# Graph network kernel: layer norm of y for every second dense step moved to where y is made

## The chip, the cores and the metric

The kernel runs on one core of a Trainium2 chip. A core has TensorE (PE), VectorE (DVE), ScalarE (ACT), GpSimd (POOL) and SyncE (SP, which here only issues DMAs), each with its own queue of instructions, and 16 DMA engines. The metric is the device time of one execution in microseconds (us); lower is better.

## The reference

Four graph layers follow one another on 50,000 nodes with 128 features, each as `x = layernorm(x + layer(x))`. The third layer, around which the change lies, is a two-step mean aggregation over 25,000 edges:

```python
def _sage(x, src, dst, Wl, b, Wr):
    m = _mean_aggr(x, src, dst, x.shape[0])
    return m @ Wl.T + b + x @ Wr.T
...
h = jax.nn.relu(_sage(x, src, dst, W1l, b1, W1r))
out = _sage(h, src, dst, W2l, b2, W2r)
...
x = _layernorm(x + _L2_gnn_ref(x, edge_index, 0, ...), axis=-1)
```

For a node that no edge ends in, the mean is zero, so its new value needs no gather: h1 = relu(x2 W1r + b1), y = x2 + h1 W2r + b2, x3 = layernorm(y).

## The kernel before, in words

Every layer treats the nodes twice. **Dense steps** compute all 50,000 nodes as if no edge ended in them: 49 steps of 128 x 8 rows, the last with 106 partitions. **Edge steps** compute the rows for the 25,000 edges, 49 steps of 128 x 4. Each table (x1, x2, h1, x3) is a DRAM tensor with the edge rows first (`SLOTS` rows) and the node rows behind them.

Each engine runs its own program. `pipeline(eng, looped, stages)` writes it: at iteration s it calls, in the order in which they are listed, all stages with their lag; a stage with lag 3 works on step s - 3. The order of the list is the order of the work on that engine, and nothing else reorders it; the engines meet by semaphores only (`wait_done`, `wait_free`, `wait_previous`, `wait_landed`, `wait_drained`). Buffers have two halves, by the step's parity `g.b`, and DMAs are counted on one semaphore for each half (`Ring`).

**The node stage** (layers `x2` and `nodes2`). One iteration makes x2 for a dense step and an edge step. SP loads node_sums and node_in (L648, L577), DVE adds the means into node_in and takes the moments (`make_x2`: L1862, L1499, L1505), ACT the root (L1197), DVE the inverse root and the shift (L1530, L1516), ACT writes the normed rows node_out (L1211) and new_rows for the edges. Two iterations later, PE transposes node_out (L1037), ACT copies it out (node_x2t, L1312), PE multiplies by W1r (L1044, the h1 product), ACT applies relu (node_h1t, L1319), PE transposes h1 back (L1063) and multiplies by W2r (L1055), ACT copies h1's rows (node_h, L1327), DVE adds ps and node_out to node_y (`nodes_y`, L1890). SP stores x2, h1 and y (L584, L654, L659); y goes to a table of its own, `y_nodes`. POOL gathers sums for the edge step (L760).

**The first aggregation** (layers `sage1` and `nodes3`). POOL gathers x2 rows (L768), DVE makes running sums and means (L1552, L1908), PE transposes and multiplies, ACT copies t_a and t_b (L1220), applies relu (L1347) and writes h1 rows (L1352). One dense step is woven into each edge step: SP loads y (L577), DVE takes moments and shifts, ACT writes eight normed rows, SP stores them to the node part of the x3 table. **The second aggregation** (`sage2`) has edge steps only.

The stages of the node stage on ACT, in this order:

```python
pipeline(act, DENSE_FULL, [
    nodes(3, nodes_copy_x2t), nodes(4, nodes_copy_h1), nodes(3, nodes_relu),
    nodes(2, normed_rows(D, "n", node_in, node_out, "n_row", "n_out", ("x2tp", "y")))]
    + edges((2, normed_rows(L, "e", pre, new_rows, "newd", "stored")))
    + [nodes(1, roots(D, "n"))] + edges((1, roots(L, "e"))))
```

## Time and profile before

| | |
|---|---|
| median of 3 runs | 3004.59 us (3003.99 to 3005.47) |
| profiled execution | 3004.84 us, its span 3003.0 us |
| PE, DVE, ACT, POOL busy, whole span | 60%, 74%, 67%, 63% |
| mean granted clock of PE | 0.772 |
| moved by DMA | 663.86 MB, 221 GB/s in the mean |

The shares of the whole span are means over stages with different limits, so a stage is read by itself: first its busy times in a window, then who waits for whom in it, then the timeline of an engine over a step. In a timeline, a row is a run of equal instructions on one engine with start, duration, and in brackets how long the engine was idle before it and what ended that. Durations overlap the next instruction's start a little; the distance between starts is what a run costs.

### The profile page before, as it was taken

To read this page: it belongs to the slowest core of one execution; us is meant where nothing else is said; L and a number is where in the kernel's file an instruction comes from. 1 tells how busy PE (TensorE), PEld (TensorE's weight loads), DVE (VectorE), ACT (ScalarE), POOL (GpSimd) and SP (SyncE) were. 2 spreads that over 40 slices of the span, in tenths; PEclk is the share of its full clock that TensorE was granted. 3 is DMA by queue.
4 is the path that set the end of the run, shared out by engine and by line. 5 is a ranking of instruction groups with operands and counts; after the bars stand their busy time and mean duration, and the time that the engine had idled before them with its cause. 6 is when DMAs were issued, how large, how long until landed. Compare 5 with 4: busy or idle time off the path is not lost. (4 is left out here: it accounts for less than half of the span.)

```text
span 3003.0 us, 51944 instructions
## 1 busy us (share of the span) xinstructions
PE 1805.3 (60%) x9371; PEld 1338.1 (45%) x9371; DVE 2230.8 (74%) x8474; ACT 2022.7 (67%) x5239; POOL 1891.8 (63%) x1802
## 2 busy tenths in 40 slices
PE   5666666444455443677777667666665666635552
PEld 4565655233333332445555433335554555524442
DVE  7978888766666663787878566666886888888883
ACT  5888878444344432788888688883554888858885
POOL 7777776588888886333333465537775766426775
PEclk8877777677767776798999888887998888755555
DMA  6989988333333333899999799996886888834441
GB/s 210 304 287 298 301 292 278 96 63 62 59 62 62 62 62 71 278 348 340 348 337 350 268 332 329 324 310 199 257 259 196 295 293 287 271 122 160 159 159 50
DMA packets 293472, 663.86 MB, mean 221 GB/s; under 512 B 55177, under 2 KB 88596, under 8 KB 293404
## 3 DMA queue, kind: packets, MB, share of 16 engines
q1 hardware_dynamic: 214587, 549.74, 52.8%
q0 software_dynamic: 78816, 113.45, 17.3%
q14 instruction: 55, 0.44, 0.0%
q8 instruction: 14, 0.23, 0.0%
HBM read 342.83 MB, written 324.08 MB: 222 GB/s over the span
## 5 line engine op out<-in xcount | busy, mean ns | idle before, releaser
L1211 ACT ACTIVATE node_out<-node_in,n_shift,n_root 128x128 f32<-128x128 f32 (+1 forms) x1176 | 468.2, 482 | 75.5 <-DVE n_shift L1516 74.6
L760 POOL DMA_INDIRECT sums<-gat_sums,dst_safe_i x196 | 185.1, 945 | 292.1 <-DVE pre L1862 237.8
L827 POOL DMA_INDIRECT gat_sums<-sums,add_idx x196 | 322.4, 1645 | 66.6 <-issue 58.5
L1499 DVE BATCH_NORM_STATS2 n_stats<-node_in 128x6 f32<-128x256 f32 (+1 forms) x784 | 279.2, 418 | 82.0 <-DMA node_in<-y_nodes 69.1
L880 POOL DMA_INDIRECT out_dram<-node_x2t,out_index x196 | 211.1, 1077 | 167.9 <-ACT node_x2t L1211 107.6
L768 POOL DMA_INDIRECT src_rows<-x_table,row_i x200 | 197.5, 988 | 134.3 <-issue 53.2
L768 POOL DMA_INDIRECT sums<-x_table,row_i x192 | 193.7, 1009 | 99.5 <-issue 50.0
L760 POOL DMA_INDIRECT own_rows<-x_table,row_i x196 | 191.1, 975 | 65.8 <-issue 54.2
L768 POOL DMA_INDIRECT own_rows<-in_x_dram,dst_safe_i x196 | 192.6, 983 | 59.7 <-issue 56.4
L760 POOL DMA_INDIRECT src_rows<-in_x_dram,src_i x196 | 191.1, 975 | 60.2 <-issue 58.7
L1220 ACT ACTIVATE t_a<-ps 128x512 f32<-128x512 f32 (+1 forms) x198 | 116.1, 587 | 149.3 <-PE ps L924 149.1
L1002 PE MATMUL ps<-node_h,msg 128*128 128x512 f32 (+1 forms) x200 | 111.6, 734 | 145.6 <-DVE node_h L1792 145.6
L1002 PE MATMUL ps<-node_y,msg 128*128 128x512 f32 (+1 forms) x192 | 106.2, 729 | 152.3 <-DVE node_y L1792 152.3
L1211 ACT ACTIVATE new_rows<-pre,e_shift,e_root 128x128 f32<-128x128 f32 x393 | 161.4, 484 | 15.1 <-DMA x_table<-new_rows 12.6
L1220 ACT ACTIVATE t_b<-ps 128x512 f32<-128x512 f32 (+1 forms) x198 | 116.0, 586 | 71.6 <-PE ps L924 71.5
L924 PE MATMUL ps<-ident,own_rows 128*128 128x128 f32 x588 | 100.4, 299 | 93.8 <-DMA own_rows<-in_x_dram,dst_safe_i 87.4
L1211 ACT ACTIVATE node_out<-node_in,n_shift,both_root 128x128 f32<-128x128 f32 (+1 forms) x392 | 156.2, 495 | 0.3 <-DVE n_shift L1516 0.3
L924 PE MATMUL ps<-ident,msg 128*128 128x128 f32 x590 | 106.1, 307 | 81.8 <-DVE msg L1908 65.2
L1002 PEld LDWEIGHTS ps<-node_h,msg 128*128 128x128 f32 x200 | 60.5, 318 | 195.3 <-issue 172.2
L1815 DVE TENSOR_TENSOR add_idx<-key,dummy_rows 128x4 int32<-128x4 f32 x49 | 8.0, 164 | 187.6 <-DMA gat_sums<-sums,add_idx 187.4
L1002 PEld LDWEIGHTS ps<-node_y,msg 128*128 128x128 f32 x192 | 57.9, 317 | 199.2 <-issue 187.2
L924 PEld LDWEIGHTS ps<-ident,msg 128*128 128x128 f32 x590 | 76.3, 158 | 140.9 <-issue 94.3
(359 smaller groups left out, 6548.7 us busy)
## 6 DMA issues: line engine op xcount, KB each, us to landing
x_table<-node_out SPq DMA_DIRECT2D x144, 512.0 KB
own_rows<-x_table SPq DMA_DIRECT2D x245, 256.0 KB, 3.0
node_in<-x_table SPq DMA_DIRECT2D x96, 512.0 KB
acc_dump<-acc SPq DMA_DIRECT2D x147, 264.0 KB
x_table<-new_rows SPq DMA_DIRECT2D x147, 256.0 KB
gat_sums<-node_x2t SPq DMA_DIRECT2D x49, 528.0 KB
node_sums<-gat_sums SPq DMA_DIRECT2D x48, 528.0 KB
node_in<-in_x_dram SPq DMA_DIRECT2D x48, 512.0 KB
```

Source lines behind the costliest of these rows:

```text
L760: g_.indirect_dma_start(out=to[:, g.b, j, 0:width], out_offset=None, in_=tab, in_offset=bass.IndirectOffsetOnAxis(ap=indices(j), axis=0)). ...
L768: g_.indirect_dma_start(out=to4[g.q][:, j, 0:F], out_offset=None, in_=tab, in_offset=bass.IndirectOffsetOnAxis(ap=indices(j), axis=0)).the ...
L827: g_.indirect_dma_start(out=gat_sums[:, :], out_offset=bass.IndirectOffsetOnAxis(ap=add_idx[:, g.b, j:j + 1], axis=0), in_=sums[:, g.b, j, ...
L880: g_.indirect_dma_start(out=out[:, :], out_offset=bass.IndirectOffsetOnAxis(ap=out_index[:, t:t + 1], axis=0), in_=wide_new[:, g.b, j, :], ...
L924: last = te.transpose(ps[bank][g.b][:, j * F:(j + 1) * F], tiles[:, j, 0:F], ident[:, :])
L1002: te.matmul(ps[2][g.b][:, 0:n], msg[:, g.b, j, 0:F], same[g.b][:, j, 0:n], start=j == J - 1, stop=j == 0)
L1211: last = sc.activation(to[0:pn, g.b, j, :], rows[0:pn, g.b, j, 0:F], ACT.Identity, bias=NORM[k][2][0:pn, g.b, j:j + 1], scale=root[0:pn, j ...
L1220: sc.activation(to[:, g.b, 0:jn * F], ps[bank][g.b][:, 0:jn * F], ACT.Copy).then_inc(L[copied].sem, 1)
L1499: last = v.bn_stats(NORM[k][0][0:pn, g.b, j:j + 2, :].rearrange("p j c -> p (j c)"), rows[0:pn, g.b, j:j + 2, 0:F].rearrange("p j f -> p f ...
L1815: v.tensor_tensor(add_idx[:, g.b, :], key4[:, g.b, 4, :], dummy_rows[:, :], ALU.add).then_inc(L["rep2"].sem, 1)
```

## The change

Every second dense step (0, 2, ... 48: 25 "even" steps) gets its layer norm in the node stage, from node_y in SBUF, and is stored straight to the x3 table instead of to `y_nodes`. The other 24 steps go to `y_nodes` as before, and only these are loaded, normed and stored in the first aggregation, one in two iterations. The result of the even norm goes to the buffer `gate`, which is free in both stages. The moments of an even step stand on DVE behind its `nodes_y`; the root, the shift and the eight rows follow an iteration later, the rows at the end of ACT's iteration, ahead of the roots. SP stores them at the head of the iteration behind that. `pipeline` learns stages at half rate, the loops of the first aggregation on SP and ACT are unrolled by four instead of two (DVE's was already), and the stages behind wait for the even stores as well.

```diff
     def at(s):
-        for lag, stage, count in stages:
-            if 0 <= s - lag < count:
-                stage(step(s - lag))
+        for lag, stage, count, *half in stages:
+            t = s - lag
+            if half and t >= 0 and t % 2 == 0 and t // 2 < count:
+                stage(step(t // 2))
+            elif not half and 0 <= t < count:
+                stage(step(t))
...
+def even_only(stage):
+    def make(g):
+        if g.b == 0:
+            stage(g, Even(g.k, 0))
+    return make
...
+            "even3": dict(front=norm("m") + ["m_row"], rings={}, steps=EVEN_STEPS),
-            "nodes3": dict(front=norm("n") + ["n_row"], rings=dict(n_in=1, n_out=1), steps=DENSE_STEPS),
+            "nodes3": dict(front=norm("n") + ["n_row"], rings=dict(n_in=1, n_out=1), steps=ODD_STEPS),
...
+        x3_even = gate[:, :, :, :].rearrange("p b j f -> p (b j) f")
...
             def store_y(g):
+                if g.b == 0:
+                    return
                 wait_done(sp, D["y"], g)
...
+            def store_even_x3(g, e):
+                wait_done(sp, flow["even3"]["m_row"], e)
+                for lo, hi in parts(g):
+                    sp.dma_start(node_rows(x3_table, SLOTS, g)[lo:hi], x3_even[lo:hi]).then_inc(even3_out, 16)
...
-            pipeline(sp, DENSE_FULL, [nodes(5, store_h1), nodes(5, store_y), nodes(3, store_nodes(D, x2_table, SLOTS))]
+            pipeline(sp, DENSE_FULL, [nodes(6, even_only(store_even_x3)), nodes(5, store_h1), nodes(5, store_y), nodes(3, store_nodes(D, x2_table, SLOTS))]
...
-                     + [nodes(0, load_nodes(D, y_nodes, 0, "n_row"))] + edges((1, dump))
-                     + [nodes(2, store_nodes(D, x3_table, SLOTS))] + edges((3, store)))
+                     + [odd_nodes(0, load_odd_y)] + edges((1, dump)) + [odd_nodes(2, store_odd_x3)] + edges((3, store)), per=4)
...
+            def even_root(g, e):
+                wait_done(act, M["m_ve"], e)
+                at = NORM["m"][1][0:dense_p(g), 0, :]
+                sc.activation(at, at, ACT.Sqrt).then_inc(M["m_rt"].sem, 1)
+
+            def even_x3(g, e):
+                pn = dense_p(g)
+                if not e.first_use():
+                    act.wait_ge(even3_out, 16 * e.k)
+                wait_done(act, M["m_nm"], e)
+                for j in range(DJ):
+                    last = sc.activation(x3_even[0:pn, j, :], node_y[0:pn, 0, j, :], ACT.Identity,
+                                         bias=NORM["m"][2][0:pn, 0, j:j + 1], scale=NORM["m"][1][0:pn, 0, j:j + 1])
+                last.then_inc(M["m_row"].sem, 1)
+
             pipeline(act, DENSE_FULL, [
-                nodes(3, nodes_copy_x2t), nodes(4, nodes_copy_h1), nodes(3, nodes_relu),
+                nodes(3, nodes_copy_x2t), nodes(5, even_only(even_root)), nodes(4, nodes_copy_h1), nodes(3, nodes_relu),
...
-                + [nodes(1, roots(D, "n"))] + edges((1, roots(L, "e"))))
+                + [nodes(5, even_only(even_x3)), nodes(1, roots(D, "n"))] + edges((1, roots(L, "e"))))
...
-            pipeline(act, DENSE_FULL, [nodes(1, roots(D, "n"))] + edges((2, h1_rows))
-                     + [nodes(1, normed_rows(D, "n", node_in, node_out, "n_row", "n_out"))]
-                     + edges((1, sage_relu), (0, sage_copies)))
+            pipeline(act, DENSE_FULL, [odd_nodes(1, roots(D, "n"))] + edges((2, h1_rows))
+                     + [odd_nodes(1, normed_rows(D, "n", node_in, node_out, "n_row", "n_out"))]
+                     + edges((1, sage_relu), (0, sage_copies)), per=4)
...
-                wait_drained(dve, D["n_y"], g)
+                if g.b:
+                    wait_drained(dve, D["n_y"], g)
+                else:
+                    wait_previous(dve, flow["even3"]["m_row"], Even(g.k, 0))
...
-            pipeline(dve, DENSE_FULL, [nodes(2, shifts(D, "n"))] + edges((2, shifts(L, "e"))) + [nodes(4, nodes_y)]
-                     + edges((1, make_x2)))
+            def even_shifts(g, e):
+                pn, at = dense_p(g), NORM["m"][1][0:dense_p(g), 0, :]
+                wait_done(dve, M["m_rt"], e)
+                v.reciprocal(at, at).then_inc(M["m_rc"].sem, 1)
+                wait_done(dve, M["m_rc"], e)
+                shift_of(M, "m", e, pn, DJ, at)
+
+            def even_moments(g, e):
+                pn = dense_p(g)
+                wait_done(dve, D["y"], g)
+                wait_previous(dve, M["m_row"], e)
+                stats(M, "m", e, node_y, pn, DJ)
+                variances(M, "m", e, pn, DJ, NORM["m"][1][:, 0, :])
+
+            pipeline(dve, DENSE_FULL, [nodes(2, shifts(D, "n"))] + edges((2, shifts(L, "e"))) + [nodes(5, even_only(even_shifts))]
+                     + [nodes(4, nodes_y), nodes(4, even_only(even_moments))] + edges((1, make_x2)))
...
-            pipeline(dve, DENSE_FULL, edges((0, plain_sums)) + [nodes(1, shifts(D, "n"))] + edges((0, means))
-                     + [nodes(0, node_moments(D))], per=4)
+            pipeline(dve, DENSE_FULL, edges((0, plain_sums)) + [odd_nodes(1, shifts(D, "n"))] + edges((0, means))
+                     + [odd_nodes(0, node_moments(D))], per=4)
```

Line numbers in the orders below are those of each program by itself: L1211 of before is L1267 of the change. The first place is ACT in the node stage, one iteration near its end, before:

```order
L1312 ACTIVATE node_x2t<-ps 128x512 x2
L1327 ACTIVATE node_h<-ps 128x512 x2
L1319 ACTIVATE node_h1t<-ps,cols 128x512 x2
L1211 ACTIVATE node_out<-node_in,n_shift,n_root 128x128 x8
L1211 ACTIVATE new_rows<-pre,e_shift,e_root 128x128 x4
L1197 ACTIVATE n_root<-n_root 106x8
L1197 ACTIVATE e_root<-e_root 128x4
```

and in the change, an iteration with an even step (m_root and gate are the root and the result of the even norm):

```order
L1368 ACTIVATE node_x2t<-ps 128x512 x2
L1392 ACTIVATE m_root<-m_root 128x8
L1383 ACTIVATE node_h<-ps 128x512 x2
L1375 ACTIVATE node_h1t<-ps,cols 128x512 x2
L1267 ACTIVATE node_out<-node_in,n_shift,n_root 128x128 x8
L1267 ACTIVATE new_rows<-pre,e_shift,e_root 128x128 x4
L1400 ACTIVATE gate<-node_y,m_shift,m_root 128x128 x8
L1253 ACTIVATE n_root<-n_root 106x8
L1253 ACTIVATE e_root<-e_root 128x4
```

One root came in behind the x2t copy, and eight row operations between new_rows and the roots.

The second place is DVE in the same stage, in the iteration in which an even y is made, of the change:

```order
L1966 TENSOR_TENSOR node_y<-ps,node_out 128x512 x2
L1572 BN_STATS m_stats<-node_y 128x6 x4
L1578 TENSOR_SCALAR m_root<-m_stats 128x8
L1923 TENSOR_REDUCE node_recip<-node_sums 128x8
L1923 TENSOR_REDUCE edge<-sums 128x4
L1928 TENSOR_SCALAR node_recip<-node_recip 128x8
L1928 TENSOR_SCALAR edge<-edge 128x4
L1931 RECIPROCAL node_recip<-node_recip 128x8
L1931 RECIPROCAL edge<-edge 128x4
L1935 SCALAR_TENSOR_TENSOR node_in<-node_sums,node_recip,node_in 128x128 x8
L1935 SCALAR_TENSOR_TENSOR pre<-sums,edge,own_rows 128x128 x4
```

The two lines with m_stats are new; the rows from node_recip on are `make_x2`, which stood directly behind node_y before.

The third place is ACT in the first aggregation, before:

```order
L1197 ACTIVATE n_root<-n_root 128x8
L1352 ACTIVATE new_rows<-ps 128x512
L1211 ACTIVATE node_out<-node_in,n_shift,n_root 128x128 x8
L1347 ACTIVATE t_c<-ps,cols 128x512
L1220 ACTIVATE t_a<-ps 128x512
L1220 ACTIVATE t_b<-ps 128x512
L1197 ACTIVATE n_root<-n_root 128x8
L1352 ACTIVATE new_rows<-ps 128x512
```

and in the change, over two iterations:

```order
L1276 ACTIVATE t_a<-ps 128x512
L1276 ACTIVATE t_b<-ps 128x512
L1425 ACTIVATE new_rows<-ps 128x512
L1420 ACTIVATE t_c<-ps,cols 128x512
L1276 ACTIVATE t_a<-ps 128x512
L1276 ACTIVATE t_b<-ps 128x512
L1253 ACTIVATE n_root<-n_root 128x8
L1425 ACTIVATE new_rows<-ps 128x512
L1267 ACTIVATE node_out<-node_in,n_shift,n_root 128x128 x8
```

The dense step's root and its eight rows (L1267) stand in every second iteration only.

## Rows read from the trace of the kernel before

**Rows 1.** Windows of three stages: us, busy per engine, clock, DMA share, GB/s

```profile
1234.60:1690.00 455.40, 343.43 (x1755) 237.24 (x1754) 367.28 (x1448) 375.92 (x921) 163.19 (x173) 0.92 0.96 343
1710.40:2019.40 309.00, 215.06 (x767) 113.70 (x768) 208.13 (x773) 259.34 (x624) 172.04 (x182) 0.85 0.95 323
2044.00:2290.00 246.00, 170.60 (x1181) 140.36 (x1179) 200.71 (x750) 129.97 (x323) 180.81 (x190) 0.96 0.80 248
```

**Rows 2.** Tile node_y: form, count, ns min/median/max, first and last start

```profile
L1890 DVE TENSOR_TENSOR node_y<-ps,node_out x98: 678/681/692, 1224.0 to 1698.4; 128x512 f32<-128x512 f32 x96, 106x512 f32<-106x512 f32 x2
```

**Rows 3.** Timeline of ACT, first aggregation's first and last t_b: start, us, operation

```profile
1710.41 0.60 ACT L1220 ACTIVATE t_b<-ps 128x512 f32<-128x512 f32 x1 [6.95 <-PE ps L924]
...
2019.36 0.58 ACT L1220 ACTIVATE t_b<-ps 128x512 f32<-128x512 f32 x1
```

**Rows 4.** Waits, 1250 to 1650 us: total us, times, longest

```profile
ACT node_h1t L1319 <- PE ps L1044: 47.3, 40, 2.8
DVE node_recip L1850 <- DMA node_in<-x_table: 43.3, 31, 2.5
...
ACT n_root L1197 <- DVE n_root L1505: 15.5, 17, 1.8
```

**Rows 5.** Timeline of ACT, one node step

```profile
1442.08 0.20 ACT L1197 ACTIVATE n_root<-n_root 128x8 f32<-128x8 f32 x1
...
1442.37 1.08 ACT L1312 ACTIVATE node_x2t<-ps 128x512 f32<-128x512 f32 x2
1443.34 1.09 ACT L1327 ACTIVATE node_h<-ps 128x512 f32<-128x512 f32 x2
1445.53 1.26 ACT L1319 ACTIVATE node_h1t<-ps,cols 128x512 f32<-128x512 f32 x2 [1.09 <-PE ps L1044]
1446.68 3.17 ACT L1211 ACTIVATE node_out<-node_in,n_shift,n_root 128x128 f32<-128x128 f32 x8
1449.76 1.64 ACT L1211 ACTIVATE new_rows<-pre,e_shift,e_root 128x128 f32<-128x128 f32 x4
```

**Rows 6.** Timeline of DVE, one node step, and ACT's root in it

```profile
1409.44 1.43 DVE L1499 BATCH_NORM_STATS2 n_stats<-node_in 128x6 f32<-128x256 f32 x4
1410.79 0.74 DVE L1499 BATCH_NORM_STATS2 e_stats<-pre 128x6 f32<-128x256 f32 x2
1411.45 0.18 DVE L1505 TENSOR_SCALAR n_root<-n_stats 128x8 f32<-128x8 f32 x1
...
1411.66 0.21 ACT L1197 ACTIVATE n_root<-n_root 128x8 f32<-128x8 f32 x1 [1.23 <-DVE n_root L1505]
...
1420.03 0.18 DVE L1505 TENSOR_SCALAR n_root<-n_stats 128x8 f32<-128x8 f32 x1
```

**Rows 7.** Timeline of PE: transposes (L1063) and h1 products (L1044)

```profile
1409.88 1.04 PE L1063 MATMUL ps<-ident,node_h1t 128*128 128x128 f32 x8
1413.05 3.68 PE L1044 MATMUL ps<-node_x2t,w1r_t 128*128 128x512 f32 x4 [2.13 <-ACT node_x2t L1312]
...
1583.56 1.98 PE L1044 MATMUL ps<-node_x2t,w1r_t 128*128 128x512 f32 x4 [1.61 <-ACT node_x2t L1312]
...
1592.66 1.98 PE L1044 MATMUL ps<-node_x2t,w1r_t 128*128 128x512 f32 x4 [0.73 <-ACT node_x2t L1312]
...
1623.28 1.98 PE L1044 MATMUL ps<-node_x2t,w1r_t 128*128 128x512 f32 x4 [2.94 <-ACT node_x2t L1312]
```

**Rows 8.** DMA issues: count, KB each, us to landing

```profile
y_nodes<-node_y SPq DMA_DIRECT2D x48, 512.0 KB, 6.1
```

**Rows 9.** Timeline of POOL, first gathers of the first aggregation

```profile
1691.75 0.94 POOL L768 DMA_INDIRECT src_rows<-x_table,row_i  x1 [27.91 <-DMA x_table<-new_rows]
1693.00 0.95 POOL L768 DMA_INDIRECT src_rows<-x_table,row_i  x1 [0.30 <-issue]
```

**Rows 10.** Timeline of ACT, second aggregation's first and last t_a

```profile
2044.35 0.60 ACT L1220 ACTIVATE t_a<-ps 128x512 f32<-128x512 f32 x1 [13.81 <-PE ps L924]
...
2293.16 0.60 ACT L1220 ACTIVATE t_a<-ps 128x512 f32<-128x512 f32 x1 [1.57 <-PE ps L924]
```

More of the change, by code:

```diff
@@ L43 @@
 WJ = 7
+ODD_STEPS, EVEN_STEPS = DENSE_STEPS // 2, DENSE_STEPS // 2 + 1
 WIDE_STEPS = T // WJ
@@ L55 @@
 MAGIC = 1597463007.0
-assert FULL_P == P - 1 and 0 < LAST_T < T and T % J == 0 and T % WJ == 0 and DENSE_FULL * P * DJ + TAIL_P * DJ == N_NODES
+assert DENSE_FULL % 2 == 0 and FULL_P == P - 1 and 0 < LAST_T < T and T % J == 0 and T % WJ == 0 and DENSE_FULL * P * DJ + TAIL_P * DJ == N_NODES
 class Step:
@@ L183, in pipeline @@
 def pipeline(eng, looped, stages, per=2):
-    longest = max(lag for lag, _, _ in stages)
+    longest = max(lag for lag, *_ in stages)
     def at(s):
-        for lag, stage, count in stages:
-            if 0 <= s - lag < count:
-                stage(step(s - lag))
+        for lag, stage, count, *half in stages:
[4 more added lines that the diff above has]
+                stage(step(t))
     first = (longest + 3) // 2 * 2 if per == 2 else (longest + 5) // 4 * 4
@@ L198, in pipeline @@
         for h in range(per):
-            for lag, stage, count in stages:
+            for lag, stage, count, *half in stages:
                 if lag + count <= first:
@@ L202, in pipeline @@
                 t = first + h - lag
-                stage(Step(i * (per // 2) + t // 2, t % 2, t % 4, i + t // 4))
-    for s in range(first + per * loops, max(lag + count for lag, _, count in stages)):
+                if not half:
+                    stage(Step(i * (per // 2) + t // 2, t % 2, t % 4, i + t // 4))
+                elif t % 2 == 0:
+                    stage(Step(i + t // 4, t // 2 % 2))
+    for s in range(first + per * loops, max(lag + count * (2 if half else 1) for lag, _, count, *half in stages)):
         at(s)
@@ L224, in wide_edges, with index, odd_nodes @@
     return [(lag, stage, WIDE_STEPS) for lag, stage in stages]
+class Odd(Step):
+    def index(self):
+        return (2 * self.k + self.b) * 2 + 1
+class Even(Step):
+    def index(self):
+        return self.k
+def odd_nodes(lag, stage):
+    return (lag, stage, ODD_STEPS, True)
+def even_only(stage):
[3 more added lines that the diff above has]
+    return make
 def once(lag, stage):
@@ L397, in gnn_program @@
         NORM = {k: (sb(f"{k}_stats", [P, 2, n, 3]), sb(f"{k}_root", [P, 2, n]),
-                    sb(f"{k}_shift", [P, 2, n])) for k, n in (("e", J), ("a", DJ), ("n", DJ))}
+                    sb(f"{k}_shift", [P, 2, n])) for k, n in (("e", J), ("a", DJ), ("n", DJ), ("m", DJ))}
         edge4 = sb("edge4", [P, 2, 6, J])
@@ L472, in gnn_program @@
                     sems[n], counts[n] = sem2(n), [0, 0]
-                flow[layer][n] = Ring(sems[n], counts[n], m, steps, n in ("n_in", "n_out", "n_h1", "n_y"))
+                flow[layer][n] = Ring(sems[n], counts[n], m, steps, n in ("n_in", "n_out", "n_h1", "n_y") and steps == DENSE_STEPS)
                 counts[n] = flow[layer][n].end
@@ L481, in gnn_program @@
                 flow[layer][n] = Signal(sem(n), 0, per)
+        flow["nodes2"]["n_y"].end[0] = 0
+        even3_out = sem("even3_out")
+        EVEN3_STORED = 16 * (EVEN_STEPS - 1 + len(TAIL_PARTS))
+        x3_even = gate[:, :, :, :].rearrange("p b j f -> p (b j) f")
         LAYER_NO = {n: i for i, n in enumerate(("msg", "sage1", "sage2", "att2"))}
@@ L670, in _, with load_odd_y, store_odd_x3 @@
             dump, store = dump_and_store(L, h1_table)
+            def load_odd_y(g):
+                wait_free(sp, D["n_row"], g)
+                sp.dma_start(node_in[:, g.b, :, :], node_rows(y_nodes, 0, Odd(g.k, g.b))).then_inc(D["n_in"].sems[g.b], 16)
+            def store_odd_x3(g):
+                wait_done(sp, D["n_row"], g)
+                sp.dma_start(node_rows(x3_table, SLOTS, Odd(g.k, g.b)), node_out[:, g.b, :, :]).then_inc(D["n_out"].sems[g.b], 16)
             pipeline(sp, DENSE_FULL, edges((0, load_own(L, L["tr_b"], x2_table, own_rows, L["own"])))
-                     + [nodes(0, load_nodes(D, y_nodes, 0, "n_row"))] + edges((1, dump))
-                     + [nodes(2, store_nodes(D, x3_table, SLOTS))] + edges((3, store)))
+                     + [odd_nodes(0, load_odd_y)] + edges((1, dump)) + [odd_nodes(2, store_odd_x3)] + edges((3, store)), per=4)
             L = flow["sage2"]
@@ L689, in _ @@
             wait_all(sp, flow["nodes3"]["n_out"])
+            sp.wait_ge(even3_out, EVEN3_STORED)
             wait_all(sp, flow["sage2"]["stored"])
@@ L864, in _ @@
             wait_all(pool, flow["nodes3"]["n_out"])
+            pool.wait_ge(even3_out, EVEN3_STORED)
             def gather_x3(g):
```

2 lines of the change are left out of this document (added).

## Prediction

> **What bounds the kernel now.** I first read the busy times by stage, because the change touches two stages only [rows 1]. In the first, which makes x2, h1 and y ("node stage", 1234.6 to 1690.0), the 16 DMA engines are busy 96% of the time at 343 GB/s, ACT 376 of 455 us (83%), DVE 367 (81%), PE 343 (75%). In the second, the first aggregation (1710.4 to 2019.4), DMA is at 95% and 323 GB/s, and ACT at 259 of 309 us (84%). The third row is the second aggregation, which has no dense steps beside it: DMA only 80%. By these shares both stages look bound by transfers. Then the length of a step: y is made 49 times, in halves, the first at 1224.0 and the last near 1698.4 [rows 2], so a node step takes 474.4/48 = 9.88 us. The first aggregation does 48 steps between its first and last copy of t_b, (2019.36 - 1710.41)/48 = 6.44 us [rows 3].
>
> Next, what each engine waits for in the node stage, over 400 us or about 40 steps [rows 4]: DVE waits 43.3 us for node_in to land, which is the transfer bound, but ACT also waits 47.3 us for PE's h1 product and only 15.5 us for DVE's variances. ACT's work of 375.92/455.4 x 9.88 = 8.2 us and its wait for PE of 47.3/40 = 1.2 us make 9.4 of the 9.88 us. The wait for PE is no spare room: it lies inside ACT's fixed order. In the timeline of ACT [rows 5] a step runs root, x2t, h copy, then 1.09 us idle while PE multiplies, relu, eight node_out, four new_rows. The shortest distance from one h1 product to the next is 1592.66 - 1583.56 = 9.10 us [rows 7]. That is ACT's own period when nothing else is late. So ACT is within 0.8 us of being the bound in every node step.
>
> **The change, node stage.** Bytes: for an even step the 512 KB store of y becomes a 512 KB store of x3 [rows 8], so the transfers of this stage stay as they are and nothing is gained here. Work is added, once in two steps.
>
> ACT gets one root and eight row operations, in the pipeline's odd iterations. Eight of the same form take 1449.76 - 1446.68 = 3.08 us start to start [rows 5]. The root of about 0.1 us goes into the wait for PE, and costs nothing unless that wait vanishes. Root and Identity already alternate here, and the order shows no table load added. The eight stand between new_rows and the roots for which DVE waits, so an odd iteration takes 9.10 + 3.08 = 12.2 us.
>
> DVE gets four moments and a variance in the even iterations, behind the halves of y and ahead of make_x2. Four moments are 1410.79 - 1409.44 = 1.35 us start to start, the variance with its wait about 0.15, so 1.5. DVE's path from ACT's root to the next variance is 1420.03 - 1411.66 = 8.4 us, and 0.2 more until ACT's root starts (1411.45 to 1411.66) [rows 6]. With 1.5 that is 10.1 us, more than ACT's 9.1. So the even iteration ends at DVE: 10.1 us. DVE's other added work (inverse root and shift, about 0.4 us, behind the wait of about 0.6 for ACT's even root) falls in the odd iteration, where DVE then needs 9.6 of 12.2 us: free.
>
> SP gets a wait for the even x3 at the head of an even iteration, with seven issues queued behind it, the loads for the step among them. Those loads are used an iteration later, and the last of them waits for node_out anyway, so I cost the wait at nothing; its cover is that iteration of 10 us. POOL's gathers of sums gain nothing and lose nothing. DVE's wait for node_in (1.1 us a step) disappears, since x2's loads now have more time; that is already in the periods above. The added wait of DVE's even y on the previous even x3 has ended by then, because ACT's roots stand behind that x3.
>
> An even and an odd iteration take 22.3 us with PE at full clock. After an odd iteration PE stands idle for about 4 us: its transposes end some 2 us behind node_out [rows 7], while new_rows, the eight and x2t fill about 6 us. In this trace the h1 product took 1.98 us in nearly all steps and 3.68 us after an idle gap of 2.13 us, though 1.98 after one of 2.94 [rows 7]: after a gap PE is sometimes at 1.2 instead of 2.4 GHz. A slow product delays ACT by 1.7 us; in the even iteration ACT then needs 10.8 and exceeds DVE by 0.7. I take that half of the time: 22.7 us. Against 19.76 that is 2.94 us, 24 times: **+70.6 us**. Bounds: always full clock 22.3 and small luck, +57; half clock in both iterations 24.1 or so, +95 with some recovery.
>
> The page "TensorE: Matmul & The Clock Gate" of the Trainium skill (section "HAM oscillation — how this bites in real kernels") says that a repeated idle stretch puts the array back to half rate, so that every group starts cold. By that rule each even iteration would start slow, a pair would be 23.0 us and the term +78; this trace agrees only in part, with 3.68 us once and 1.98 us after a longer gap.
>
> **The change, first aggregation.** It loses 25 of 49 loads of y and 25 of 49 stores of x3, 512 KB each: of some 2.1 MB a step (rate times 6.44 us) about a quarter. The rest, 2.08 - 0.53 = 1.55 MB, takes 4.8 us at 323 GB/s. ACT loses 3.2 us and DVE about 1.9 us in every second step. What is next: POOL's gathers come every 1693.00 - 1691.75 = 1.25 us at best [rows 9], four a step, 5.0 us. The nearest row is the second aggregation, with the same gathers and without dense steps: 48 steps from 2044.35 to 2293.16 [rows 10], 5.18 us each. ACT's work without the dense part is 259.34/48 - 3.2 = 2.2 us [rows 1], so steps with dense work need 3.2 + 2.2 and small waits, about 5.5 us, steps without it about 4.6 (copies, PE's product and transposes in a loop); their mean is near 5.1, and POOL's four buffers let them average. Transfers would be at some 93%. I take 5.2: (6.44 - 5.2) x 48 = **-59.4 us**. Bounds: POOL's 196 gathers at 1.25 us from 1691.75 end at 1937, and some 8 us behind them is 1945, so -74; and 5.6 us a step if PE's product takes 3.7 us in the light steps, -40.
>
> **Ends.** Between the stages SP now passes the store of the last even x3 instead of waiting for y; both are due at about the same time. At the end of the aggregation no dense step is in the way of the last relu: **-1.5 us**.
>
> **Sum.** 70.6 - 59.4 - 1.5 = +9.7 us. The profiled execution took 3004.84 us (span 3003.0), 0.25 above the median of 3004.59, and the sum is made against it: 3014.5 us. About 0.2% (6 us) is what a measurement can tell from no change.
>
> **The rivals.**
> (a) *Forecast*: ACT paces the node stage, the aggregation goes to about 5.2 us. Chance 0.45.
> (b) *The other side: ACT's idle time takes up the work.* The node stage stays bound by transfers. ACT's work for two steps would be 2 x 8.2 + 3.2 = 19.6 us, just under the 19.76 that the unchanged bytes need, so the stage costs nothing: 3004.8 - 59.4 - 1.5 = 2944 us; at half of the added time, 2979. It decides where ACT's wait for PE can be filled. Against it: the order puts the eight behind new_rows, not into that wait. Chance 0.08.
> (c) *The gathers set the aggregation*, with PE at full clock: +57 - 74 - 2, 2986 us. For it: the step without dense work in the second aggregation stands at 5.18 with two loads of own rows. Chance 0.12.
> (d) *PE's clock falls more often*, in the node stage (+95) and in part of the light steps (-50): 3004.8 + 95 - 50 - 1.5 = 3048 us. For it: more idle time of PE; the clock is 0.92 in the node stage and 0.85 in the aggregation [rows 1]. Against it: the second aggregation, also with gaps, has 0.96. The rule of the page named above is the mild form of this. Chance 0.20.
> (e) *The aggregation is held by its latencies*, landing of loads and stores, not by bytes: 5.9 us a step, 26 us saved: 3004.8 + 70.6 - 26 - 1.5 = 3048 us. For it: with its period above what PE and ACT need, its waits can re-form. Against it: the 5.18 us of the second aggregation. Chance 0.15.
>
> **How the numbers follow.** Faster by over 0.2%: (b), (c) and a sliver of (a), 0.22. Slower by over 0.2%: (d), (e) and two thirds of (a), 0.64. Within: 0.14. The range runs from (c) to (d) and (e): 2984 to 3050, which leaves out (b) and the worst of (d). The likeliest case's own range is 3003 to 3028.
>
> **What would show it.** The y of the node stage should come alternately some 10.1 to 10.8 and 12.2 us apart, 11.3 in the mean; DVE's wait for node_in should be near nothing; DMA in that stage should fall from 96% to about 85%. The first aggregation should take about 250 us from its first copy to its last instead of 309, with DMA at 90% or more and POOL's idle time mostly "issue". It would be wrong if the node stage kept 9.9 us a step (b), or if the aggregation stayed above 5.6 (d, e).

## Result and profile after

| | before | after |
|---|---|---|
| median of 6 runs each | 3005.32 us (3003.99 to 3019.88) | 3035.8 us (3028.39 to 3041.04) |
| profiled execution, its span | 3004.84, 3003.0 us | 3036.36, 3034.6 us |
| ACT busy, whole span | 2022.7 us | 2016.6 us |
| moved by DMA | 663.86 MB | 637.84 MB |

The ratio after to before is 1.0088 (95%: 1.0069 to 1.0107): slower, by 31.6 us of span between the two profiles, where +9.7 was forecast. The direction held, and ACT's added rows pace the stage as forecast; one term was too small by 24 us. Ratios compare the fast runs alone, medians take in all: now and then an execution ran longer at a lower clock, as did five of the twelve runs of the last kernel of this document, its profiled one among them.

The stages, as windows of the profile of the changed kernel (columns as in [rows 1]):

```profile
1234.60:1785.00 550.40, 390.01 (x1754) 258.83 (x1753) 409.64 (x1607) 444.52 (x1128) 163.66 (x174) 0.82 0.81 284
1804.80:2050.00 245.20, 188.19 (x756) 107.46 (x756) 163.75 (x600) 179.84 (x405) 172.26 (x182) 0.89 0.91 303
```

In the node stage DMA fell from 96 to 81%, ACT went from 83 to 81%, and PE's clock from 0.92 to 0.82: neither transfers nor ACT's own work fill the time. The first aggregation became much shorter, with transfers still at 91%.

The ends of the stages, for [rows 2, 3, 10]: the tile node_y, and copies in the timeline of ACT (start, length):

```profile
L1966 DVE TENSOR_TENSOR node_y<-ps,node_out x98: 680/682/692, 1223.9 to 1792.9; 128x512 f32<-128x512 f32 x96, 106x512 f32<-106x512 f32 x2
```

```profile
1806.43 0.60 ACT L1276 ACTIVATE t_b<-ps 128x512 f32<-128x512 f32 x1 [5.58 <-PE ps L980]
...
2053.17 0.60 ACT L1276 ACTIVATE t_b<-ps 128x512 f32<-128x512 f32 x1
...
2075.13 0.60 ACT L1276 ACTIVATE t_a<-ps 128x512 f32<-128x512 f32 x1 [13.89 <-PE ps L980]
```

From them the balance (each a difference of starts):

| stretch | before | after | difference | forecast |
|---|---|---|---|---|
| first y to last y | 474.4 | 569.0 | +94.6 | +70.6 |
| last y to first t_b | 12.0 | 13.5 | +1.5 | with the next |
| 49th t_b to second aggregation's first t_a | 25.0 | 22.0 | -3.0 | -1.5, both |
| first t_b to 49th t_b | 308.95 | 246.74 | -62.2 | -59.4 |
| sum | | | +30.9 of 31.6 | +9.7 |

The waits from 1250 to 1700 us (total us, times, longest; [rows 4] are of 400 us, these of 450):

```profile
POOL sums L815 <- DVE pre L1935: 263.0, 37, 8.8
...
PE ps L1100 <- ACT node_x2t L1368: 73.9, 33, 3.8
ACT node_h1t L1375 <- PE ps L1100: 63.3, 38, 2.9
DVE n_root L1603 <- ACT n_root L1253: 62.8, 38, 3.2
...
ACT node_x2t L1368 <- PE ps L1093: 17.6, 12, 2.2
...
ACT n_root L1253 <- DVE n_root L1578: 4.7, 6, 1.2
...
DVE node_recip L1923 <- DMA node_in<-x_table: 3.2, 5, 0.7
```

DVE no longer waits for transfers (43.3 us before, 3.2 now) but for ACT's roots, which stand behind the eight new rows. ACT waits 63.3 us for PE's h1 product in 38 steps, where it was 47.3 in 40, and one wait grew that the forecast's account doesn't have: ACT's copy of x2t waits for PE's transposes of x2 (L1093), 17.6 us in all and up to 2.2 at a time, where before it was 5.4 us and at most 0.7:

```profile
ACT node_x2t L1312 <- PE ps L1037: 5.4, 11, 0.7
```

PE itself waits up to 3.8 us for ACT, and POOL 263.0/37 = 7.1 us at a time for DVE.

Now the timelines, of PE (for [rows 7]) and of ACT (for [rows 5]; the eight added rows go under the name gate):

```profile
1430.59 1.16 PE L1111 MATMUL ps<-w2r_t,node_h1t 128*128 128x128 f32 x8
1431.94 1.09 PE L1093 MATMUL ps<-ident,node_out 128*128 128x128 f32 x8 [0.19 <-ACT node_out L1267]
1432.87 1.04 PE L1119 MATMUL ps<-ident,node_h1t 128*128 128x128 f32 x8
1437.70 3.78 PE L1100 MATMUL ps<-node_x2t,w1r_t 128*128 128x512 f32 x4 [3.80 <-ACT node_x2t L1368]
1443.37 2.08 PE L1111 MATMUL ps<-w2r_t,node_h1t 128*128 128x128 f32 x8
...
1449.73 1.98 PE L1100 MATMUL ps<-node_x2t,w1r_t 128*128 128x512 f32 x4 [0.30 <-ACT node_x2t L1368]
...
1461.90 3.78 PE L1100 MATMUL ps<-node_x2t,w1r_t 128*128 128x512 f32 x4 [3.80 <-ACT node_x2t L1368]
1467.57 2.08 PE L1111 MATMUL ps<-w2r_t,node_h1t 128*128 128x128 f32 x8
1470.11 2.08 PE L1111 MATMUL ps<-w2r_t,node_h1t 128*128 128x128 f32 x8
1471.98 1.91 PE L1093 MATMUL ps<-ident,node_out 128*128 128x128 f32 x8
1473.69 1.45 PE L1119 MATMUL ps<-ident,node_h1t 128*128 128x128 f32 x8
1475.07 1.98 PE L1100 MATMUL ps<-node_x2t,w1r_t 128*128 128x512 f32 x4
```

```profile
1413.71 0.19 ACT L1253 ACTIVATE n_root<-n_root 128x8 f32<-128x8 f32 x1
...
1424.15 0.21 ACT L1253 ACTIVATE n_root<-n_root 128x8 f32<-128x8 f32 x1 [1.25 <-DVE n_root L1578]
...
1431.78 1.64 ACT L1267 ACTIVATE new_rows<-pre,e_shift,e_root 128x128 f32<-128x128 f32 x4
1433.32 3.18 ACT L1400 ACTIVATE gate<-node_y,m_shift,m_root 128x128 f32<-128x128 f32 x8
1436.39 0.20 ACT L1253 ACTIVATE n_root<-n_root 128x8 f32<-128x8 f32 x1
...
1436.59 1.06 ACT L1368 ACTIVATE node_x2t<-ps 128x512 f32<-128x512 f32 x2
...
1441.52 1.26 ACT L1375 ACTIVATE node_h1t<-ps,cols 128x512 f32<-128x512 f32 x2 [2.91 <-PE ps L1100]
...
1473.93 1.08 ACT L1368 ACTIVATE node_x2t<-ps 128x512 f32<-128x512 f32 x2 [2.15 <-PE ps L1093]
```

While ACT does the eight (3.07 us start to start), PE has nothing: idle 3.80 us, and the next product takes 3.78 us instead of 1.98, half rate (1.2 GHz). In the pair that begins with the product at 1461.90 the half rate lasts on through both y products (2.08 instead of 1.16) and the transposes of x2 (1.91 instead of 1.09), and so ACT's x2t waits 2.15 us more. This even iteration takes 1475.07 - 1461.90 = 13.17 us.

Over all 24 pairs, from product to product: the odd iteration takes 12.17 to 12.18 us in all but the first, as forecast (12.2). The even one takes 11.63 in the mean, where 10.1 at full clock and 10.8 at half were forecast, and 10.45 taken. By what was slow in them, the even iterations fall into three groups:

| even iterations | count | their length, us |
|---|---|---|
| opening product at full rate (the second y product slow in all four) | 4 | 9.59, then 10.52 three times |
| only the opening product slow (3.25 to 3.48 us) | 4 | 10.53 to 10.60 |
| product slow, and a y product behind it too | 16 | 11.06 to 13.17, mean 12.23 |

In 13 of the 16 both y products are slow (2.08 us for most), and in 13 of the 16 the transposes of x2 are (1.6 to 2.0 us). From 1415 us on the lengths recur as 10.52, 12.0, 13.17, 12.3, 10.59 us. In all the opening product was slow in 20 of 24 (2.85 to 3.78 us); the first even iteration had no long gap ahead of it, so it is 20 of 23 behind a gap, 18 of 21 behind one of 3.80 us and 2 of 2 behind one of about 2.5.

### The profile page after: what moved, and what is told of

The parts are those of the page before. It is cut to its first block, busy times and chain, and to the rows that moved or that the text cites. A ratio compares the mean times of both kernels' runs of the same rounds, so it can differ in the third digit from the quotient of the medians.

```text
span 3034.6 us, 51718 instructions
## 1 busy us (share of the span) xinstructions
PE 1824.2 (60%) x9371; PEld 1355.4 (45%) x9371; DVE 2233.7 (74%) x8474; ACT 2016.6 (66%) x5239; POOL 1890.4 (62%) x1802
## 2 busy tenths in 40 slices
DMA packets 286297, 637.84 MB, mean 210 GB/s; under 512 B 54356, under 2 KB 87775, under 8 KB 286227
## 4 chain that ended last, share of the span: by engine, by line
ACT 17%; PE 14%; DVE 10%; issue 10%; DMA 6%; DVEq 1%; POOL 1%; SPq 1%; ACTq 1%; POOLq 0%
ACT node_out L1267 6%; PE ps L1100 4%; DMA acc_dump<-acc 4%; PE ps L1111 2%; DVE n_stats L1572 2%; ACT node_x2t L1267 2%; ACT gate L1400 2%; DVE node_in L2067 2%; ACT node_x2t L1368 1%; ACT new_rows L1267 1%; PE ps L1093 1%; ACT node_h1t L1375 1%; PE ps L1144 1%; DVE msg L1823 1%; PE ps L1145 1%
## 5 line engine op out<-in xcount | busy, mean ns | idle before, releaser
L1267 ACT ACTIVATE node_out<-node_in,n_shift,n_root 128x128 f32<-128x128 f32 (+1 forms) x976 | 388.6, 483 | 56.2 <-DVE n_shift L1589 55.3
L1572 DVE BATCH_NORM_STATS2 n_stats<-node_in 128x6 f32<-128x256 f32 (+1 forms) x684 | 243.5, 419 | 40.1 <-DMA node_in<-y_nodes 27.1
L1100 PE MATMUL ps<-node_x2t,w1r_t 128*128 128x512 f32 x196 | 127.5, 785 | 96.0 <-ACT node_x2t L1368 95.9
L1267 ACT ACTIVATE new_rows<-pre,e_shift,e_root 128x128 f32<-128x128 f32 x393 | 161.4, 484 | 16.0 <-DMA x_table<-new_rows 13.4
L1267 ACT ACTIVATE node_out<-node_in,n_shift,both_root 128x128 f32<-128x128 f32 (+1 forms) x392 | 156.3, 496 | 0.3 <-DVE n_shift L1589 0.3
```

What stands on the lines that cost most here:

```text
L1100: last = te.matmul(ps[1][h][:, :], w1r_t[:, :], node_x2t[:, g.b, h * J * F:(h + 1) * J * F], start=True, stop=True)
L1267: last = sc.activation(to[0:pn, g.b, j, :], rows[0:pn, g.b, j, 0:F], ACT.Identity, bias=NORM[k][2][0:pn, g.b, j:j + 1], scale=root[0:pn, j ...
L1572: last = v.bn_stats(NORM[k][0][0:pn, g.b, j:j + 2, :].rearrange("p j c -> p (j c)"), rows[0:pn, g.b, j:j + 2, 0:F].rearrange("p j f -> p f ...
```

## Experiments

Lengths of the node stage (first y to last y) and of the first aggregation (first to 49th t_b), from each kernel's profile; ratios are to the kernel before, run on the same chip. All of them test one theory: ACT's eight rows in the odd iteration, and the idle time of PE that they make, set the node stage.

### PE kept at work in the gap

```diff
                 for j, bank, i, _ in by_bank(pn):
                     last = te.transpose(ps[2][bank][0:pn, i * F:(i + 1) * F], node_h1t[:, g.b, j * F:j * F + pn], ident[:, :])
+                if g.b == 0:
+                    for _ in range(3):
+                        for j, bank, i, _c in by_bank(pn):
+                            last = te.transpose(ps[2][bank][0:pn, i * F:(i + 1) * F], node_h1t[:, g.b, j * F:j * F + pn], ident[:, :])
                 last.then_inc(D["h1tp"].sem, 1)
```

> The change, with PE's back-transposes of h1 done four times over instead of once where the step is even, so that PE has some 3 us more to do in the stretch in which it stood idle for 3.8 us ahead of the even iteration's h1 product; same results. Node stage = first to last y, 474.4 us before, 569.0 with the change. Theory (the clock falls in that gap and costs the even iterations more than I took): every product takes 1.98 us, the even iterations 10.5 us, the odd ones stay at 12.2, the stage takes about 545 us and the whole 3036 - 24 = 3012 us. Rival (the even iterations are long by DVE's moments, or by SP's wait for the even x3): the products get fast, the stage stays above 562 us, the whole at 3030 us or more.

Measured: 3018.83 us (10 runs), ratio 1.0026 (1.0009 to 1.0043), where the change has 1.0088; node stage 548.7 us instead of 569.0, aggregation 248.9. PE's timeline with the filler (L1123):

```profile
1500.25 2.78 PE L1123 MATMUL ps<-ident,node_h1t 128*128 128x128 f32 x24
1504.22 1.98 PE L1100 MATMUL ps<-node_x2t,w1r_t 128*128 128x512 f32 x4 [1.19 <-ACT node_x2t L1372]
...
1514.74 3.19 PE L1100 MATMUL ps<-node_x2t,w1r_t 128*128 128x512 f32 x4 [2.15 <-ACT node_x2t L1372]
...
1529.28 1.88 PE L1100 MATMUL ps<-node_x2t,w1r_t 128*128 128x512 f32 x4
```

In windows from 1234.6 to 1700 us the clock is 0.91 with the filler and 0.83 without. The gap ahead of an even iteration's product is down to 1.19 us, that product is at 1.98 us, and the iteration takes 10.52 us as a rule, 9.0 to 9.4 in some. But ahead of an odd iteration's product there is still a gap of 2.15 us, and there a product is slow at times: 3.19 us at 1514.74, and that iteration takes 1529.28 - 1514.74 = 14.54 us. A pair takes 22.99 us in the mean (10.10 and 12.89), against 23.85 (11.63 and 12.22). So the even iterations gave back 36.7 us and the odd ones took 16.1 of it again; in those of 14.54 us the next product starts right behind the filler, without a gap, so part of their length is the filler's own work. The half rate behind the gap is a cause, worth at least the 20 us that came back; less idle time thinned the slow stretches out and moved them, and didn't end them.

### One of the eight rows on ACT, and one of four moments on DVE

Two kernels, each beside the other:

```diff
-                for j in range(DJ):
+                for j in range(1):
                     last = sc.activation(x3_even[0:pn, j, :], node_y[0:pn, 0, j, :], ACT.Identity,
```

> The change with one row operation of ACT instead of eight for an even x3 (seven of eight parts of the even x3 rows are left out). Theory (the eight on ACT's order are the price, and the gap of PE's clock comes with them): odd iterations fall from 12.2 to about 9.9, even ones to 10.1 to 10.5, the node stage to 485 to 495 us, the whole to about 2955 us. Rival (the wait of SP at the head of the even iteration, or DVE's moments, hold the stage): the stage stays above 520 us.

```diff
-                at = NORM["m"][1][0:dense_p(g), 0, :]
+                at = NORM["m"][1][0:dense_p(g), 0, 0:2]
...
-                                         bias=NORM["m"][2][0:pn, 0, j:j + 1], scale=NORM["m"][1][0:pn, 0, j:j + 1])
+                                         bias=NORM["m"][2][0:pn, 0, j % 2:j % 2 + 1], scale=NORM["m"][1][0:pn, 0, j % 2:j % 2 + 1])
...
-                stats(M, "m", e, node_y, pn, DJ)
-                variances(M, "m", e, pn, DJ, NORM["m"][1][:, 0, :])
+                stats(M, "m", e, node_y, pn, 2)
+                variances(M, "m", e, pn, 2, NORM["m"][1][:, 0, :])
```

> The change with one of DVE's four moments for an even step (two of eight rows' moments, used for all eight; moments of the others left out). Theory (half of the even iterations or more are held by ACT and a slow PE, not by DVE): 24 x 0.3 to 0.5, some 7 to 12 us less in the node stage, about 560 us. Rival (DVE sets the even iterations): 24 x 1.1 = 26 us less, 543 us.

Measured, one run each, on the chip of the kernel with the filler: with one row 2956.01 us, node stage 493.1, iterations of 10.36 and 10.34 us; with one moment 3025.42 us, stage 562.7. Seven rows are worth 75.9 us of stage. ACT's own time for them is 7 x 0.385 x 24 = 65 us, but that isn't what came back where they stood: the odd iterations fell by 24 x (12.22 - 10.36) = 44.7 us, until something else held them, and the even ones, in which these rows don't stand, by 24 x (11.63 - 10.34) = 31 us: the price of the slow stretches in them, as the filler shows too. Three moments are worth 6.3. What they hold is seen where the opening product is at full rate: that iteration takes 9.88 us without them instead of 10.52. ACT's rows are the change's price; DVE's share is small as long as ACT stands above it.

### The eight rows in ACT's wait for PE

```diff
-                nodes(3, nodes_copy_x2t), nodes(5, even_only(even_root)), nodes(4, nodes_copy_h1), nodes(3, nodes_relu),
+                nodes(3, nodes_copy_x2t), nodes(5, even_only(even_root)), nodes(4, nodes_copy_h1), nodes(5, even_only(even_x3)), nodes(3, nodes_relu),
...
-                + [nodes(5, even_only(even_x3)), nodes(1, roots(D, "n"))] + edges((1, roots(L, "e"))))
+                + [nodes(1, roots(D, "n"))] + edges((1, roots(L, "e"))))
```

> The change with ACT's eight rows of the even x3 moved from the end of its odd iteration to between the h copy and relu, where it waits about 1.0 us for PE; same results. Theory (ACT's own order is the bound of odd iterations): odd ones go from 12.2 to 11.2 us, and PE's gap ahead of the even product shrinks from 3.8 to about 1 us, so even ones go to 10.5: node stage 24 x 21.7 = 521 us, the whole 3036 - 48 = 2988 us. Rival (the slow clock moves along: PE now idles for 3 us between product and y in odd iterations, and y or the transposes come late): the stage stays at 545 us or more.

Measured: 2997.48 us (10 runs), ratio 0.9952 (0.9937 to 0.9967); stage 533.2, aggregation 243.5. The order alone turned the change from slower to faster. The even iteration takes 9.67 us, the odd one 12.52. PE's timeline of an odd iteration's relu, and ACT's next copy:

```profile
1506.84 0.60 PE L1109 MATMUL ps<-b_parts,ones_bf 3*128 3x512 bf16 x1 [3.30 <-ACT node_h1t L1375]
1507.38 2.08 PE L1111 MATMUL ps<-w2r_t,node_h1t 128*128 128x128 f32 x8
```

```profile
1513.16 1.08 ACT L1368 ACTIVATE node_x2t<-ps 128x512 f32<-128x512 f32 x2 [1.57 <-PE ps L1093]
```

The wait for PE is filled with work, but PE now idles 3.30 us in another place, ahead of the y products, and these run at half rate (2.08 us). So the odd iteration fell short of the 11.2 us expected: ACT gives back 1.57 us at x2t. All h1 products but the stage's first are at 1.98 us. The stage lies between the 521 us of the theory and the 545 of its rival.

### The eight rows on POOL; a split of the rows; and neither

The POOL kernel takes the eight from ACT and puts them behind POOL's gathers, five steps late:

```diff
+            def pool_even_x3(s):
...
+                wait_done(pool, M["m_nm"], e)
+                for j in range(DJ):
+                    last = g_.tensor_scalar(x3_even[0:pn, j, :], node_y[0:pn, 0, j, :], NORM["m"][1][0:pn, 0, j:j + 1],
+                                            NORM["m"][2][0:pn, 0, j:j + 1], ALU.mult, ALU.add)
+                last.then_inc(M["m_row"].sem, 1)
+
+            for s in range(STEPS + 7):
+                if s < STEPS:
+                    gather_sums(step(s))
+                pool_even_x3(s - POOL_LAG)
```

> The change with the eight row operations of an even x3 on POOL instead of ACT (tensor_scalar with the same two columns, behind the step's four gathers); ACT keeps the even root; same results. POOL is busy for 4 of about 12 us a step there, and what one of the eight costs on it no run shows: I take 0.3 to 0.8 us, up to 6.4 us in 20. Theory (the loss was the place on ACT and the clock that goes with it, so it disappears with them): odd iterations 9.9 us, even ones 10.3 as in the run with one row on ACT, node stage 485 to 500 us, the aggregation unchanged at about 247 us, the whole 2950 to 2965 us, 1.6% under the kernel before. Rival (POOL's operations slow DVE's beside them, or come late for the gathers): stage above 520 us.

The next leaves out what the two cut kernels above leave out, together (one row, one moment):

> The change with one of DVE's four moments and one of ACT's eight rows for an even step; the rest of the even norm is left out. Theory (the transfers of this stage are unchanged, and DVE's moments hold the even iterations once ACT's rows are gone): the node stage goes back to 474 to 480 us, against 493 us with all four moments; the whole 2935 to 2945 us, which is what half rate in the aggregation is worth alone. Rival (SP's wait or its additional wait for the even store hold something): stage stays at 490 us or more.

And the split: rows 0 to 2 stand between the h copy and relu, rows 3 to 7 where the change has all eight.

```diff
...
+            def even_first(g, e):
+                even_x3(g, e, range(3))
...
-                nodes(3, nodes_copy_x2t), nodes(5, even_only(even_root)), nodes(4, nodes_copy_h1), nodes(3, nodes_relu),
+                nodes(3, nodes_copy_x2t), nodes(5, even_only(even_root)), nodes(4, nodes_copy_h1), nodes(5, even_only(even_first)), nodes(3, nodes_relu),
...
```

> The change with the eight rows split: three between h copy and relu, where ACT waits about 1.0 us for PE, five at the end as in the change; same results. Theory (both ACT's order and PE's gaps count; three fill the wait and open no gap of PE, five leave one of about 2.6 us): odd iterations 11.2 us, even ones 10.5 in most: node stage about 522 us, below the 533 of all eight in the wait; the whole 0.8% under the kernel before. Rival (only the length of ACT's order counts): stage 533 us as with all eight there, or more.

These ran on a chip on which the kernel before takes 3352.91 us (12 runs). There: POOL 3389.19, ratio 1.0107 (1.0079 to 1.0136); one row and one moment 3352.19 (one run); split 3388.49, ratio 1.0108 (1.0066 to 1.015). Node stages 521.3, 508.5 and 525.6 us, aggregations 351.3, 351.4 and 355.7. What differs between the chips is seen in a window that the change doesn't touch, 40 to 520 us, of the same POOL kernel on this chip and on the one of the next comparison:

```profile
40.00:520.00 480.00, 270.26 (x1635) 249.30 (x1636) 320.65 (x1157) 312.57 (x971) 306.61 (x302) 0.77 0.74 234
```

```profile
40.00:520.00 480.00, 314.99 (x2043) 279.83 (x2044) 396.36 (x1441) 393.58 (x1208) 360.43 (x369) 0.78 0.90 296
```

234 GB/s against 296, at the same clock, and fewer steps done in the time. That says nothing on the question, so the three ran again elsewhere, with the change beside them.

> The kernel of e5_pool once more, since in that comparison all kernels, the one before too, took 3335 us and more, with transfers slower in every stage. Eight rows on POOL take 4.2 us there (1518.93), 0.52 each. Theory, where the kernel before takes about 3005 us: node stage 485 to 500 us, aggregation about 247 us, the whole 2950 to 2965 us. Rival (POOL's rows come late, or slow DVE): stage above 520 us.

> The kernel of e6_no_even once more (one moment, one row; the rest of the even norm left out). Theory: node stage 474 to 480 us, the whole 2935 to 2945 us, what half rate in the aggregation is worth alone. Rival (SP's wait or the additional waits hold something): 490 us or more.

> The kernel of e7_split once more (three rows in ACT's wait for PE, five at the end). In the slower comparison its iterations came out at 10.44 and 11.63 us, the second between 11.04 and 12.4 with PE's slow stretches. Theory: 24 x 22.07 = 530 us for the node stage, about 533 as with all eight in the wait, the whole 0.4 to 0.8% under the kernel before. Rival (the gap left to PE still drops the clock as in the change): above 545 us.

> The change itself, beside the other three on the same chip: node stage 565 to 573 us, aggregation 245 to 249 us, the whole 3025 to 3042 us.

| kernel | us | ratio to before (3011.54, 7 runs) | node stage | first aggregation |
|---|---|---|---|---|
| change | 3034.43 (1 run) | | 569.4 | 243.3 |
| split | 2986.3 (4) | 0.9912 (0.9894 to 0.993) | 524.9 | 248.7 |
| rows on POOL | 2969.9 (4) | 0.9868 (0.9848 to 0.9887) | 497.5 | 245.3 |
| one row, one moment | 2957.37 (1) | | 491.5 | 245.4 |

The version with the rows on POOL beats both kernels here: 1.3% under before, with the whole of the computation done. Its iterations are 10.64 and 10.24 us. POOL's timeline, and its waits from 1300 to 1700 us:

```profile
1505.50 0.94 POOL L816 DMA_INDIRECT sums<-gat_sums,dst_safe_i  x1 [0.30 <-issue]
1506.74 0.95 POOL L816 DMA_INDIRECT sums<-gat_sums,dst_safe_i  x1 [0.30 <-DVE m_shift L1605]
1507.73 4.17 POOL L908 TENSOR_SCALAR gate<-node_y,m_root,m_shift 128x128 f32<-128x128 f32 x8
1513.34 0.97 POOL L816 DMA_INDIRECT sums<-gat_sums,dst_safe_i  x1 [1.44 <-DVE pre L1951]
```

```profile
ACT node_h1t L1394 <- PE ps L1119: 41.9, 38, 2.0
...
ACT n_root L1272 <- DVE n_root L1594: 31.3, 36, 1.4
...
DVE n_root L1619 <- ACT n_root L1272: 9.7, 35, 0.9
```

POOL needs 4.17 us for the eight and still waits 1.44 us for its next gather, so they are hidden. The order of the waits turned round: ACT waits for DVE (31.3 us) and DVE hardly for ACT (9.7 in these 400 us, where the change has 62.8 in 450). The end of the stage gets longer: from the last y to the first t_b it is 20.8 us here and 13.5 in the change. POOL's first gather of the aggregation stands behind its last eight rows, 6.8 us behind the last y; in the change it starts 7.5 us ahead of it.

The kernel with one row and one moment was a miss: 474 to 480 us of stage were expected, DVE's four moments being taken for the second bound, and it has 491.5, only 1.6 under the 493.1 of one row alone (another chip, of nearly the same time for before). So some 17 us of stage over the 474.4 of before belong neither to ACT's rows nor to DVE's moments. Candidates are the remaining row and chain of roots, and DVE's wait for ACT's even root, 19.8 us in 400 in its profile. Its waits from 1300 to 1700 us name one more, the transfers:

```profile
DVE node_recip L1923 <- DMA node_in<-x_table: 22.1, 14, 2.4
DVE m_root L1975 <- ACT m_root L1392: 19.8, 19, 2.7
```

The wait for node_in, 3.2 us in the change, is half back to the 42.3 us that the kernel before has in this window, with DMA at 92%; all 14 of these waits stand in every second iteration, where before they stood in both kinds. The granted clock is 0.89 here, 0.92 before and 0.83 in the change. SP's wait for x3, ahead of the step's stores and loads, is a fourth candidate and a weaker one: it is 21.2 us in 19 times, 1.3 at most, and behind it SP waits longer for ACT's node_out, ahead of the load of node_in, 117.5 us in 38 times. None of these was taken away by itself, and this stays open.

One last kernel moves DVE's even shift behind the halves of y in the POOL version:

```diff
-            pipeline(dve, DENSE_FULL, [nodes(2, shifts(D, "n"))] + edges((2, shifts(L, "e"))) + [nodes(5, even_only(even_shifts))]
-                     + [nodes(4, nodes_y), nodes(4, even_only(even_moments))] + edges((1, make_x2)))
+            pipeline(dve, DENSE_FULL, [nodes(2, shifts(D, "n"))] + edges((2, shifts(L, "e"))) 
+                     + [nodes(4, nodes_y), nodes(5, even_only(even_shifts)), nodes(4, even_only(even_moments))] + edges((1, make_x2)))
```

> The kernel of e8_pool_again with DVE's inverse root and shift of an even step moved behind nodes_y instead of ahead of it, so that DVE no longer stands waiting for ACT's even root (14.0 us in 400 there, 0.7 in every second step); same results. Theory (with ACT relieved, DVE's path sets both iterations, and every wait on it counts): the node stage goes from 497.5 to about 485 us, the whole to about 0.4% below that kernel, 1.7% below the kernel before. Rival (SP's longer chain of issues or the transfers hold the stage now): the node stage stays at 494 us or more.

It ran on a chip with slow transfers again (before 3351.75 us, 17 runs): 3379.44 (12 runs), ratio 1.0041 (1.0007 to 1.0075). The ratio lies below the POOL version's 1.0107 (1.0079 to 1.0136), but that was another such chip, and the ratio is of seven of its runs, 3350 to 3380 us; the other five took 3400 to 3419. Its stage is 512.5 us, where the POOL version had 521.3, and its aggregation 369.9 where that had 351.3, but the profile is of one of those five (3400.4 us). Inconclusive: it hints at 9 us in the stage, of the 12 expected on a chip with fast transfers, and doesn't show them.

## Why the forecast was right in kind and short in size

- **ACT becomes the bound of the odd iteration, 12.2 us**: right to 0.02 us, and the seven rows' removal shows that it is those rows (493.1 us of stage).
- **DVE bounds the even iteration at 10.1 us**: the right bound, 0.4 low. From ACT's root at 1413.71 to its next at 1424.15, which waited for DVE, it is 10.44 us. It decides only where PE's slow stretch doesn't reach past the product.
- **The step that failed: "A slow product delays ACT by 1.7 us ... I take that half of the time: 22.7 us."** The term is too small by 24 us, and neither the share of slow products nor the price of one is what it lacks in the main. They were slow in 20 of 24 pairs and not in half, but one that is slow alone costs what the forecast gives it, 9.10 + (3.47 - 1.98) = 10.59 us, and that is 0.07 over the 10.52 that DVE sets. What the step left out is that the half rate goes on behind the product: in 16 even iterations a y product is slow too, in 13 of them the transposes as well, and these 16 take 12.23 us in the mean. 16 x (12.23 - 10.45) = 28 us is all that the distances of products have above the forecast, since the other eight take 10.43 in the mean; by the starts of y 24 are missing between +70.6 and +94.6, and the two differ at the ends of the stage.
- **The row used for the 1.7 us shows it already, before any change.** Behind the product of 3.68 us at 1413.05 [rows 7] the second y product takes 1.97 us and the transposes of x2 1.91, and the next h1 product comes 11.61 us later, not 10.8:

```profile
1418.40 1.16 PE L1055 MATMUL ps<-w2r_t,node_h1t 128*128 128x128 f32 x8
...
1419.81 1.97 PE L1055 MATMUL ps<-w2r_t,node_h1t 128*128 128x128 f32 x8
1421.57 1.91 PE L1037 MATMUL ps<-ident,node_out 128*128 128x128 f32 x8
1423.28 1.08 PE L1063 MATMUL ps<-ident,node_h1t 128*128 128x128 f32 x8
1424.66 1.98 PE L1044 MATMUL ps<-node_x2t,w1r_t 128*128 128x512 f32 x4 [0.30 <-ACT node_x2t L1312]
```

- The upper bound of +95 was reached, by another way than it was made: not half rate in both iterations but a longer half rate in one. That it fits to 1 us is luck. The row on which the half was based [rows 7] came after a gap of 2.13 us; the gap that the change makes, which the text put at about 4 us, had no row of its own, and the nearest, 1.98 us behind 2.94, spoke against what came.
- The page "TensorE: Matmul & The Clock Gate" of the Trainium skill (section "HAM oscillation — how this bites in real kernels") has each group behind a repeated idle stretch start cold, which gave +78. The trace agrees for 20 of 23 groups behind a gap, and measures more, +94.6, since the slow stretch here reached past the product that the +78 priced.
- **First aggregation -59.4**: -62.2, 5.14 us a step for 5.2 taken. Transfers are at 91%, and POOL's idle time is "issue" (24.7 and 24.1 us in the window from 1820 to 2040 us). ACT does wait for PE's products there, 50.9 us in 22 times, but the steps stayed at 5.14 us and not at the 5.6 of the -40 bound.
- **Transfers of the node stage no longer bind, DVE's wait for node_in goes**: 3.2 us left of 43.3, and DMA at 81% for the 85 forecast.
- **Ends -1.5**: +1.5 and -3.0, the same.
- **SP's added wait costs nothing**: not settled. In the change SP does wait for the even x3, 64.6 us in 17 times from 1300 to 1700 us, and DVE's wait for node_in is 3.2 us all the same, which speaks for it. But with nearly all of the added work of ACT and DVE taken out, 17 us of node stage remain, no kernel leaves out this wait alone, and DVE's wait for node_in is back.
- Of the rivals, (d), PE's clock falling more often, is the one that came in the node stage, and only there; (b) is refuted for the change, but its condition, that ACT's wait be filled, is what the kernel with the rows in that wait meets in part (2997.48 us, where (b) gave 2944 to 2979). (e) is refuted by the 5.14 us a step; (c) is near in the aggregation, where POOL issues gathers almost without waiting, but not at its -74.

## What to carry to other kernels

Work added to an engine in a ring of engines costs its own time and the idle time that it makes next door: read the gap that it opens on PE, and price PE's whole next group at half rate, not its first product. Before giving such work to the engine that already paces the stage, look for one whose waits are longer than the work: here POOL's waits of 7.1 us took 4.17 us of rows, and 3034 us became 2970 on one chip, against 3012 of the kernel before; on a chip with slower transfers the same version was the slower one, by 1.0107. Where the work must stay, its place in the order counts: moving the eight into ACT's wait gave 35.8 us of stage, about half of the 75.9 that leaving out seven of them gave.

## Unexpected of the hardware

- The same kernel moved 234 GB/s on one chip and 296 on another in the same stretch, and on these two chips the kernel before took 3353 and 3012 us. The gain from the POOL version changed its sign with it, 1.0107 against 0.9868. The aggregation takes some 351 us there and 245 here in the same kernel. Why the sign flips wasn't tested, since the kernel before has no profile on the slower chip.
- From 1415 us on, PE's half rate comes in a pattern over five pairs of iterations that hardly varies (10.52, 12.0, 13.17, 12.3, 10.59 us), although each odd iteration leaves the same gap of 3.80 us. A slow product of 3.47 us can cost nearly nothing (10.59 against 10.52), where one of 3.78 costs up to 2.65 us.
- Eight rows of 128x128 with two column operands take 3.07 us on ACT (1433.32 to 1436.39) and 4.17 us on POOL (at 1507.73; 3.46 for the eight at 1714.84, at the end of the stage).
